# Fewer semaphore updates from TensorE in a two-layer graph network kernel: three a chunk in stage 0 instead of six, one a pair of turns in stage 1

## The chip, the cores and the metric

The kernel runs on one core of a Trainium2 chip. The metric is the time of one execution on the device in microseconds; the kernel before has a median of 1814.22 us in 3 runs. The engines are TensorE (PE, with its weight loads PEld), VectorE (DVE), ScalarE (ACT), GpSimd (POOL) and SyncE (SP, which issues DMAs). Each has an instruction stream of its own, and they keep in step by semaphores: an instruction adds to a semaphore when it is done (`then_inc`), and another engine waits until the semaphore has reached a count (`wait_ge`).

## The reference

Two message-passing layers over 3125 nodes with 64 channels and 100000 edges that are sorted by their destination. Each layer is followed by a sum with its input and a layer norm.

```python
# layer 0
h1, h2, h3, h4 = node_proj(x, W1..W4, b1..b4, node_type)
w5e = einsum('mf,mfh->mh', edge_attr_16, W5[edge_type]) + b5[edge_type]
num = sum(h3[dst] * (h4[src] + w5e), axis=-1)
score = softmax((num / 4)[:, None], axis=-1)[:, 0]   # over an axis of one element
out = h1 + segment_sum(score[:, None] * (h2[src] + w5e), dst)
x = layernorm(x + out)
# layer 1
m = relu(x[src] + edge_attr_32 @ We + be) + 1e-7
ez = exp(m - segment_max(m, dst)[dst])
a = ez / segment_sum(ez, dst)[dst]
x = layernorm(x + ((x + segment_sum(m * a, dst)) @ Wm + bm))
```

## The kernel before

After a setup (node projections, index lists, zeroing of a table in HBM) come two long loops, one for each layer, called stage 0 and stage 1 here. Each goes over 98 chunks. A chunk is 2 x 512 edges: partitions 0 to 63 hold the 64 channels of 512 edges of the first half of the edge list, partitions 64 to 127 those of the second half. Buffers come in pairs; `s = c % 2` picks one and `r = c // 2` counts its uses, so a semaphore `name[s]` reaches `r + 1` when chunk c has signalled.

The order of work on each engine is written out by hand: a `for` over c, and within it a tuple of (work, d), where `d` shifts the chunk that this work is done for. Nothing is reordered by a compiler; an engine whose next instruction waits stands still.

**Stage 0, TensorE** (loop at L934): `pick0` gathers some h rows by one-hot matmuls (L872, three 125x512 bf16 matmuls for each of some 6.9 tiles). `project0` multiplies the edge features by W5 (L881) and adds the gathered h4 rows by transposes into `q_sum` (L854, L859). `turn_inj` transposes the injected h3 rows (L894), `numerator` the products (L909); `difference` adds the other rows to `q_sum` (L854, L859 again), so that this then holds the message part q2; `turn_prob` transposes the widened scores (L918) and `turn_run` the running sums (L927). Each ends with an update: q4_ready, injT, num_ready, q2_ready, probT and runT.

**Stage 0, VectorE** (L1240): `score_parts` of c-1 reduces the turned products (L1184, L1187, L1190); `mask` of c+1 (L1196); `expand` of c is a scan that spreads h3 over the edges (L1205); `products` of c (L1213); `probabilities` of c-1 (L1218 to L1223); `message_sums` of c-2 is a multiplication and a scan (L1229, L1235); `one_hot0` makes about seven one-hot tiles for `pick0` (L1178).

**Stage 0, ScalarE** (L720): `exponents` of c-1, `copy_keep` of c (L690, after the scan of c-2 is done), `widen` of c-1 (L683, what `turn_prob` turns), `copy_q2` of c (L696), at times `copy_picked`, and `store0` of c-2 (L713), which copies the turned running sums out of PSUM and sends them to HBM. GpSimd issues the gathers (`gather0`, L599); eight buffers of a ring are reused once `q2_ready` of the chunk eight back is there.

**Stage 1**: VectorE runs `maxima` (L1328, L1333, L1337), `summands` (L1343), one-hot tiles (L1285) and `sums`, two scans (L1353 and L1358). TensorE picks by one-hot (L970), projects (L949, L952, L958) and then `turn1` turns both running sums: four transposes of the first into the left half of `p_out1`, four of the second into the right half (all L981). ScalarE's `store1` copies the halves out in two instructions (L789), behind `decay` (L776) and ahead of `messages` (L759, L761) of three chunks later.

Of the kernel before, what the change touches and what calls it, by code (L numbers as in the profile page):

```python
# [28 lines left out]
P = 128  # L29
# [50 lines left out]
def gnn_program(nc, t, out):  # L80
# [3 lines left out]
    with ctx:  # L84
# [204 lines left out]
        feat_in, keep_in, inj_in = sems("feat_in"), sems("keep_in"), sems("inj_in")  # L289
        masked, q4_ready, q2_ready, injT = sems("masked"), sems("q4_ready"), sems("q2_ready"), sems("injT")  # L290
        keep_copied, q2_copied, h3_ready, prod_ready = sems("keep_copied"), sems("q2_copied"), sems("h3_ready"), sems("prod_ready")
        num_ready, score_ready, diff_ready = sems("num_ready"), sems("score_ready"), sems("diff_ready")
        exps_ready, prob_ready = sems("exps_ready"), sems("prob_ready")
        softmax_step = sems("softmax_step")
        wide_ready, probT, msg_ready = sems("wide_ready"), sems("probT"), sems("msg_ready")
        run_ready, runT, staged, stored = sems("run_ready"), sems("runT"), sems("staged"), sems("stored")
        s_cut, s_square, s_squared, s_var, s_sqrt, s_x1, s_x1_out = (sem("s_cut"), sem("s_square"), sem("s_squared"),
# [354 lines left out]
        def _(act):  # L652
# [57 lines left out]
            def store0(s, r, c):  # L710
                act.wait_ge(runT[s], r + 1)
                wait(act, stored[s], 16 * r)
                act.activation(stage0[s][:, :, :].rearrange("p j c -> p (j c)"), p_out0[:, :], ACT.Copy).then_inc(staged[s], 1)  # L713
                act.wait_ge(staged[s], r + 1)
                act.dma_start(d_run0[bass.ds(2 * CH * c, 2 * CH), :].rearrange("(p j h) c -> p j (h c)", j=TILES, h=2),
                              stage0[s][:, :, :]).then_inc(stored[s], 16)
# [68 lines left out]
            def store1(s, r, c):  # L785
                act.wait_ge(stored[s], 16 * (EACH + r))
                for q in range(2):
                    act.wait_ge(runT[s], EACH + 2 * r + q + 1)
                    act.activation(stage1[s][:, :, :, q, :], p_out1[:, q * CH:(q + 1) * CH].rearrange("p (j h c) -> p j h c", j=TILES, h=2),  # L789
# [27 lines left out]
        def _(pe):  # L817
# [59 lines left out]
            def project0(s, r, c):  # L877
# [5 lines left out]
                if c in PICKED:  # L883
                    n = PICKED.index(c)
                    pe.wait_ge(own_ready[n // 2 % 2], n // 4 + 1)
                add_rows(s, c, 1).then_inc(q4_ready[s], 1)

# [10 lines left out]
            def difference(s, r, c):  # L898

                pe.wait_ge(prod_ready[s], r + 1)  # L900
                add_rows(s, c, 0).then_inc(q2_ready[s], 1)

            def numerator(s, r, c):
# [4 lines left out]
                for j in range(TILES):  # L908
                    ins = pe.matmul(p_num[:, j * P:(j + 1) * P], prod[s][:, j:CH:TILES], ident[:, :], is_transpose=True,  # L909
                                    start=True, stop=True)  # L910
                ins.then_inc(num_ready[s], 1)

# [9 lines left out]
            def turn_run(s, r, c):  # L922
# [3 lines left out]
                for j in range(TILES):  # L926
                    ins = pe.matmul(p_out0[:, j * P:(j + 1) * P], run[s][:, j:CH:TILES], ident[:, :], is_transpose=True,  # L927
                                    start=True, stop=True)
                ins.then_inc(runT[s], 1)

# [3 lines left out]
            for c in range(-1, CHUNKS - 2):  # L934
                if AHEAD_PIECES + c + 1 < len(PIECES):
                    pick0(AHEAD_PIECES + c + 1)
                for work, d in ((project0, 1), (turn_inj, 1), (numerator, 0), (difference, 0), (turn_prob, -1), (turn_run, -2)):
                    if chunk_of(c + d):
                        work(*chunk_of(c + d))
            for work, back in ((numerator, 2), (difference, 2), (turn_prob, 3), (turn_run, 4), (turn_inj, 1), (project0, 1),  # L940
                               (turn_prob, 2), (numerator, 1), (difference, 1), (turn_run, 3), (turn_run, 2), (turn_prob, 1), (turn_run, 1)):
                work(*chunk_of(CHUNKS - back))
# [32 lines left out]
            def turn1(s, r, c):  # L975
                for q, (src, ready) in enumerate(((run_s[s], s_run[s]), (run_n[s], n_run[s]))):
# [3 lines left out]
                    for j in range(TILES):  # L980
                        ins = pe.matmul(p_out1[:, q * CH + j * P:q * CH + (j + 1) * P], src[:, j:CH:TILES], ident[:, :],  # L981
                                        is_transpose=True, start=True, stop=True)
                    ins.then_inc(runT[s], 1)

# [41 lines left out]
        def _(dve):  # L1026
# [154 lines left out]
            def score_parts(s, r, c):  # L1181

                dve.wait_ge(num_ready[s], r + 1)
                dve.tensor_reduce(score[s][:, :, :, :].rearrange("p j h a -> p (j h a)"), p_num[:, :].rearrange("p (e c) -> p e c", c=C),  # L1184
# [7 lines left out]
            def mask(s, r, c):  # L1192

                dve.wait_ge(feat_in[s], 16 * 4 * (r + 1))
                wait(dve, q4_ready[s], r)
                dve.scalar_tensor_tensor(featm[s][:, :], types[s][:, :], type_of_row[:, :], feat[s][:, :],  # L1196
# [11 lines left out]
            def products(s, r, c):  # L1208

                dve.wait_ge(h3_ready[s], r + 1)  # L1210
                dve.wait_ge(q4_ready[s], r + 1)
                wait(dve, num_ready[s], r)
                dve.scalar_tensor_tensor(prod[s][:, :], h3d[s][:, :], 0.25, q_sum[s], ALU.mult, ALU.mult).then_inc(prod_ready[s], 1)  # L1213
# [11 lines left out]
            def message_sums(s, r, c):  # L1225
# [6 lines left out]
                if c > 0:  # L1232
                    dve.wait_ge(run_ready[1 - s], r + s)
                wait(dve, runT[s], r)
                dve.tensor_tensor_scan(run[s][:, :], keep_late[s][:, :], p_prob[:, :], run[1 - s][:, CH - 1:CH],  # L1235
# [110 lines left out]
            def sums(s, r, c):  # L1346

                first = c == 0
                dve.wait_ge(decay_ready[s], r + 1)
                dve.wait_ge(runT[s], EACH + 2 * r)  # L1350
                if not first:
# [120 lines left out]
```

## Time and profile before

| | us |
|---|---|
| runs, median of 3 (lowest, highest) | 1814.22 (1812.03, 1814.47) |
| profiled execution, span | 2243.3 |
| TensorE matmuls busy | 1756.8 (78%) |
| VectorE busy | 1622.9 (72%) |
| GpSimd busy | 1321.5 (59%) |
| ScalarE busy | 785.0 (35%) |

The profiled execution is one execution under the hardware profiler, and all rows below come from it. It takes 429 us longer than the median of the runs, so a wait seen in it need not be in the runs. Matmuls are pipelined: a busy share of TensorE counts overlapping instructions once, and the end of a matmul is modelled. In a wait, "remote" stands for a releaser that the profile doesn't know, "issue" for a wait in which nothing is shown that the engine waited for.

### The profile page before, as it was taken

Reading aid. Unit: us, or ns where it says so; the run is one execution under the profiler, and the core shown is the slowest. Engines: PE = TensorE matmul, PEld = TensorE weight load, DVE = VectorE, ACT = ScalarE, POOL = GpSimd, SP = SyncE. Lnnn points to the kernel's source line nnn. Section 1 sums busy time; section 2 is a strip of 40 time slices with the busy share of each in tenths; the row PEclk is TensorE's granted clock in tenths of the full one; section 3 lists DMA queues with packets and bytes.
Section 4 is the critical chain, followed back from the end, with each engine's and each line's share of the span. In section 5 each row is a group of like instructions: output and inputs, shape, how many; then the busy total and the mean of one; then the engine's idle time right before and its main releaser. Section 6 shows DMA issues by size and latency. Waiting matters only on the chain.

```text
span 2243.3 us, 28657 instructions
## 1 busy us (share of the span) xinstructions
PE 1756.8 (78%) x8720; PEld 1065.5 (47%) x8720; DVE 1622.9 (72%) x3313; ACT 785.0 (35%) x1508; POOL 1321.5 (59%) x1377
## 2 busy tenths in 40 slices
PE   4447988888788887889875278888888889888864
PEld 4423555555555554555544135444444545445434
DVE  6042777778777777777768558788878878879785
ACT  3110222222222222223222135555545545455551
POOL 5661566666666666666650666666666666666624
PEclk9988998999999999999987579899998999999875
DMA  7951454445454544545443235555545555555441
GB/s 252 342 129 48 124 144 131 146 138 151 135 142 146 141 148 138 148 140 147 139 128 111 53 86 154 149 152 157 157 144 158 161 141 169 150 162 155 142 145 44
DMA packets 216628, 322.18 MB, mean 144 GB/s; under 512 B 62017, under 2 KB 124026, under 8 KB 216347
## 3 DMA queue, kind: packets, MB, share of 16 engines
q1 hardware_dynamic: 128556, 147.55, 22.1%
q0 software_dynamic: 44016, 70.01, 13.6%
q10 hardware_dynamic: 43904, 102.79, 13.0%
q8 instruction: 71, 1.16, 0.2%
q14 instruction: 81, 0.66, 0.1%
HBM read 186.93 MB, written 133.22 MB: 143 GB/s over the span
## 4 chain that ended last, share of the span: by engine, by line
PE 32%; DVE 25%; issue 17%; another core or an unknown queue 15%; ACT 8%; ACTq 1%; POOL 1%; DMA 1%; DVEq 0%; SPq 0%; POOLq 0%
PE wide L970 13%; PE wide L872 5%; DVE h3d L1205 4%; PE wide L981 4%; DVE run L1235 4%; DVE late L1178 4%; DVE edge_lists L1178 3%; DVE score L1184 2%; PE bank L949 2%; DVE prod L1213 2%; ACT block L789 2%; DVE bank L1229 2%; PE bank L958 2%; PE bank L833 1%
## 5 line engine op out<-in xcount | busy, mean ns | idle before, releaser
L609 POOL DMA_INDIRECT rows<-d_x,idx x588 | 558.8, 950 | 323.0 <-issue 154.1
L599 POOL DMA_INDIRECT block<-d_h,idx x496 | 476.4, 960 | 265.0 <-issue 131.4
L970 PE MATMUL wide<-late,ntype_i 125*128 125x512 bf16 x975 | 235.2, 399 | 51.1 <-DVE ntype_i L1318 49.7
L872 PE MATMUL wide<-late,typed 125*128 125x512 bf16 x728 | 234.2, 403 | 39.0 <-issue 19.7
L599 POOL DMA_INDIRECT rows<-d_h,idx x176 | 169.0, 960 | 155.2 <-PE wide L859 51.7
L970 PE MATMUL wide<-edge_lists,ntype_i 125*128 125x512 bf16 x936 | 233.4, 406 | 9.6 <-issue 9.4
L872 PE MATMUL wide<-edge_lists,typed 125*128 125x512 bf16 x672 | 210.8, 395 | 2.8 <-issue 2.7
L981 PE MATMUL wide<-ident,block 128*128 128x128 f32 x784 | 147.3, 317 | 73.1 <-issue 56.5
L789 ACT ACTIVATE block<-wide 128x512 f32<-128x512 f32 x196 | 108.3, 592 | 266.8 <-remote 214.1
L1184 DVE TENSOR_REDUCE score<-bank 128x8 f32<-128x512 f32 x98 | 67.4, 688 | 177.9 <-remote 165.7
L690 ACT ACTIVATE keep_late<-keep 128x512 bf16<-128x512 bf16 x98 | 61.7, 630 | 353.1 <-DVE run L1235 240.8
L970 PEld LDWEIGHTS wide<-late,ntype_i 125*128 125x128 bf16 x975 | 100.1, 103 | 168.6 <-DVE ntype_i L1318 50.1
L696 ACT ACTIVATE q_sb<-wide 128x512 f32<-128x512 f32 x98 | 58.4, 596 | 299.8 <-remote 270.6
L981 PEld LDWEIGHTS wide<-ident,block 128*128 128x128 f32 x784 | 115.9, 210 | 99.6 <-issue 80.4
L970 PEld LDWEIGHTS wide<-edge_lists,ntype_i 125*128 125x128 bf16 x936 | 97.5, 104 | 130.0 <-issue 42.0
L918 PE MATMUL bank<-ident,prob_wide 128*128 128x128 f32 x392 | 67.5, 298 | 113.8 <-issue 84.6
L872 PE MATMUL wide<-late,ntype_i 125*128 125x512 bf16 x364 | 145.4, 400 | 5.4 <-issue 5.2
L872 PEld LDWEIGHTS wide<-late,typed 125*128 125x128 bf16 x728 | 74.4, 103 | 128.4 <-issue 63.0
L872 PE MATMUL wide<-edge_lists,ntype_i 125*128 125x512 bf16 x336 | 132.1, 393 | 2.0 <-issue 2.0
L1205 DVE TENSOR_TENSOR_SCAN h3d<-keep,h3d,bank 128x512 f32<-128x512 bf16 x98 | 124.8, 1274 | 8.7 <-PE bank L894 8.7
L1178 DVE TENSOR_SCALAR late<-msg,pick_of 125x512 bf16<-125x512 f16 x364 | 113.8, 376 | 21.0 <-PE wide L872 10.8
L1333 DVE TENSOR_TENSOR_SCAN h3d<-bank,h3d,keep 128x511 f32<-128x511 f32 x98 | 125.5, 1281 | 3.5
(227 smaller groups left out, 3503.6 us busy)
## 6 DMA issues: line engine op xcount, KB each, us to landing
d_run<-block ACTq DMA_DIRECT2D x98, 512.0 KB
d_inj<-zeros SPq DMA_DIRECT2D x28, 896.0 KB
inj<-d_inj SPq DMA_DIRECT2D x98, 256.0 KB
d_run<-stage ACTq DMA_DIRECT2D x98, 256.0 KB
feat<-in_ea16x3T SPq DMA_DIRECT2D x196, 96.0 KB
types<-d_type SPq DMA_DIRECT2D x196, 64.0 KB
keep<-d_keep SPq DMA_DIRECT2D x196, 64.0 KB
keep<-d_pen SPq DMA_DIRECT2D x196, 64.0 KB
```

What stands on the lines that cost most here:

```text
L599: pool.indirect_dma_start(out=ring[c % RING][:, j, h, :], out_offset=None, in_=d_h24, in_offset=bass.IndirectOffsetOnAxis(ap=idx[:, c, at: ...
L609: pool.indirect_dma_start(out=rows1[c % RING1][:, j, h, :], out_offset=None, in_=d_x1, in_offset=bass.IndirectOffsetOnAxis(ap=idx[:, c, at ...
L789: act.activation(stage1[s][:, :, :, q, :], p_out1[:, q * CH:(q + 1) * CH].rearrange("p (j h c) -> p j h c", j=TILES, h=2), ACT.Copy).then_ ...
L872: ins = pe.matmul(p_pick[s][:, 0:cols], table0[n][:, k, :], hot0[b][:, k - b * KT, 0:cols], start=(k == 0 and n == 0), stop=(k == NT - 1 a ...
L918: ins = pe.matmul(p_prob[:, j:CH:TILES], prob_wide[s][:, j, :, :].rearrange("p h c -> p (h c)"), ident[:, :], is_transpose=True, start=Tru ...
L970: ins = pe.matmul(p_hot[s], table[q][:, SPLIT * k:SPLIT * (k + 1), :].rearrange("p b c -> p (b c)"), hot[s][:, k, :], start=(k == 0 and q ...
L981: ins = pe.matmul(p_out1[:, q * CH + j * P:q * CH + (j + 1) * P], src[:, j:CH:TILES], ident[:, :], is_transpose=True, start=True, stop=True)
L1178: ins = dve.tensor_scalar(hot0[b][:, k - b * KT, 0:cols], pick_slots[u % SLOTS][0:NP, 0:cols], pick_of[:, k:k + 1], None, ALU.is_equal)
L1184: dve.tensor_reduce(score[s][:, :, :, :].rearrange("p j h a -> p (j h a)"), p_num[:, :].rearrange("p (e c) -> p e c", c=C), AX.X, ALU.add) ...
L1205: dve.tensor_tensor_scan(h3d[s][:, :], keep[s][:, :], p_inj[:, :], h3d[1 - s][:, CH - 1:CH], ALU.mult, ALU.add).then_inc(h3_ready[s], 1)
L1235: dve.tensor_tensor_scan(run[s][:, :], keep_late[s][:, :], p_prob[:, :], run[1 - s][:, CH - 1:CH], ALU.mult, ALU.add).then_inc(run_ready[s ...
L1333: dve.tensor_tensor_scan(before[s][:, 1:CH], p_m[c % 3][:, 0:CH - 1], keep[s][:, 1:CH], before[s][:, 0:1], ALU.max, ALU.add).then_inc(befo ...
```

## The change

In stage 0 three kinds of update go from TensorE's stream, or nearly: `num_ready` is dropped, `q4_ready` and `runT` are given for the last chunk alone (as `last_rows` and `last_turned`), so that three a chunk are left (injT, q2_ready, probT). Who waited for one of the dropped waits for a later instruction of the same engine:

- `score_parts` (VectorE) waits for `q2_ready`, so for `difference` as well as `numerator`; `products` waits for `q2_ready` of two chunks back where it waited for `num_ready`, and for `q4_ready` no more (its scan has waited for `injT`, which comes after the rows); `mask` waits for `injT` of two chunks back.
- `message_sums` no longer waits for `runT` of two chunks back.
- `store0` (ScalarE) of a chunk waits for `probT` of the next chunk. For this, TensorE does `turn_run` of c-2 ahead of `turn_prob` of c-1, and in the written-out end of the loop likewise.
- `difference` (TensorE) drops its wait for `prod_ready`, which `numerator` ahead of it has.

In stage 1 `turn1` updates one semaphore after all eight transposes (`turned`) where it updated `runT` after each four; `store1` waits for it once ahead of both copies, and `sums` waits for it. No matmul, copy or DMA is added or removed.

```diff
             def store0(s, r, c):
-                act.wait_ge(runT[s], r + 1)
+                if c == CHUNKS - 1:
+                    act.wait_ge(last_turned, 1)
+                else:
+                    act.wait_ge(probT[1 - s], r + s + 1)
...
             def store1(s, r, c):
                 act.wait_ge(stored[s], 16 * (EACH + r))
+                act.wait_ge(turned[s], r + 1)
                 for q in range(2):
-                    act.wait_ge(runT[s], EACH + 2 * r + q + 1)
...
-                add_rows(s, c, 1).then_inc(q4_ready[s], 1)
+                ins = add_rows(s, c, 1)
+                if c == CHUNKS - 1:
+                    ins.then_inc(last_rows, 1)
...
             def difference(s, r, c):
-                pe.wait_ge(prod_ready[s], r + 1)
                 add_rows(s, c, 0).then_inc(q2_ready[s], 1)
...
             def numerator(s, r, c):
...
-                ins.then_inc(num_ready[s], 1)
...
             def turn_run(s, r, c):
...
-                ins.then_inc(runT[s], 1)
+                if c == CHUNKS - 1:
+                    ins.then_inc(last_turned, 1)
...
-                for work, d in ((project0, 1), (turn_inj, 1), (numerator, 0), (difference, 0), (turn_prob, -1), (turn_run, -2)):
+                for work, d in ((project0, 1), (turn_inj, 1), (numerator, 0), (difference, 0), (turn_run, -2), (turn_prob, -1)):
...
             def turn1(s, r, c):
...
-                    ins.then_inc(runT[s], 1)
+                ins.then_inc(turned[s], 1)
...
             def score_parts(s, r, c):
-                dve.wait_ge(num_ready[s], r + 1)
+                dve.wait_ge(q2_ready[s], r + 1)
...
             def mask(s, r, c):
                 dve.wait_ge(feat_in[s], 16 * 4 * (r + 1))
-                wait(dve, q4_ready[s], r)
+                wait(dve, injT[s], r)
...
             def products(s, r, c):
                 dve.wait_ge(h3_ready[s], r + 1)
-                dve.wait_ge(q4_ready[s], r + 1)
-                wait(dve, num_ready[s], r)
+                if c == CHUNKS - 1:
+                    dve.wait_ge(last_rows, 1)
+                wait(dve, q2_ready[s], r)
...
             def message_sums(s, r, c):
-                wait(dve, runT[s], r)
...
             def sums(s, r, c):
-                dve.wait_ge(runT[s], EACH + 2 * r)
+                wait(dve, turned[s], r)
```

## Rows read from the trace of the kernel before

**Rows 1.** The page: span, and the chain that ended last, by engine.
```profile
span 2243.3 us, 28657 instructions
...
PE 32%; DVE 25%; issue 17%; another core or an unknown queue 15%; ACT 8%; ACTq 1%; POOL 1%; DMA 1%; DVEq 0%; SPq 0%; POOLq 0%
```

**Rows 2.** Windows of the two loops: engines' busy us (instructions), clock, DMA share, GB/s.
```profile
300.00:1100.00 800.00, 688.97 (x3688) 426.11 (x3687) 614.10 (x1384) 221.22 (x471) 506.19 (x527) 0.96 0.49 142
1320.00:2120.00 800.00, 682.01 (x3230) 386.82 (x3228) 647.38 (x1144) 410.18 (x707) 506.26 (x535) 0.91 0.53 153
```

**Rows 3.** The same windows for VectorE's L1184 alone, then for L1353 alone.
```profile
300.00:1100.00 800.00, 53.08 (x77) 0.96 0.49 142
...
1320.00:2120.00 800.00, 111.70 (x88) 0.91 0.53 153
```

**Rows 4.** Waits of stage 0's window: engine, line, releaser, us in total, times, longest.
```profile
ACT q_sb L696 <- remote: 222.3, 68, 6.3
...
DVE score L1184 <- remote: 146.3, 61, 5.4
...
POOL block L599 <- remote: 96.9, 48, 2.6
```

**Rows 5.** Timeline of TensorE's matmuls: start us, us, engine, line, count, idle before.
```profile
611.53 1.02 PE L881 MATMUL wide<-featm,w 128*128 128x512 f32 x2
...
612.97 0.60 PE L894 MATMUL bank<-ident,inj 128*128 128x128 f32 x4
613.40 0.64 PE L909 MATMUL bank<-ident,prod 128*128 128x128 f32 x4
613.88 0.52 PE L854 MATMUL wide<-ident,block 128*128 128x128 f32 x3
614.24 0.39 PE L859 MATMUL wide<-typed,ident 128*128 128x128 f32 x2
616.87 0.66 PE L918 MATMUL bank<-ident,prob_wide 128*128 128x128 f32 x4 [2.24 <-issue]
617.36 0.65 PE L927 MATMUL bank<-ident,run 128*128 128x128 f32 x4
617.85 0.38 PE L872 MATMUL wide<-edge_lists,typed 125*128 125x512 bf16 x1
```

**Rows 6.** Timeline of VectorE, the chunk that follows.
```profile
618.57 0.69 DVE L1184 TENSOR_REDUCE score<-bank 128x8 f32<-128x512 f32 x1 [0.89 <-remote]
619.29 0.16 DVE L1187 TENSOR_REDUCE top<-score 128x8 f32<-128x8 f32 x1
...
621.55 0.69 DVE L1213 SCALAR_TENSOR_TENSOR prod<-h3d,wide 128x512 f32<-128x512 f32 x1
622.15 0.15 DVE L1218 TENSOR_REDUCE total<-expo 128x8 f32<-128x8 f32 x1
...
623.39 1.28 DVE L1235 TENSOR_TENSOR_SCAN run<-keep_late,run,bank 128x512 f32<-128x512 bf16 x1
624.59 2.17 DVE L1178 TENSOR_SCALAR late<-msg,pick_of 125x512 bf16<-125x512 f16 x7
```

**Rows 7.** Timeline of ScalarE and GpSimd at the same place.
```profile
615.67 0.63 ACT L690 ACTIVATE keep_late<-keep 128x512 bf16<-128x512 bf16 x1 [4.43 <-DVE run L1235]
...
618.64 0.60 ACT L696 ACTIVATE q_sb<-wide 128x512 f32<-128x512 f32 x1 [1.82 <-remote]
...
618.87 0.94 POOL L599 DMA_INDIRECT block<-d_h,idx  x1 [1.83 <-remote]
```

**Rows 8.** Timeline of TensorE in stage 1: the turns of a chunk, then the picks.
```profile
1703.61 1.13 PE L981 MATMUL wide<-ident,block 128*128 128x128 f32 x8
...
1704.58 4.70 PE L970 MATMUL wide<-late,ntype_i 125*128 125x512 bf16 x21
```

**Rows 9.** Waits of stage 1's window.
```profile
ACT block L789 <- remote: 207.4, 53, 8.1
...
DVE h3d L1328 <- ACT bank L761: 96.3, 17, 9.3
```

More of the change, by code:

```diff
@@ L289, in gnn_program @@
         feat_in, keep_in, inj_in = sems("feat_in"), sems("keep_in"), sems("inj_in")
-        masked, q4_ready, q2_ready, injT = sems("masked"), sems("q4_ready"), sems("q2_ready"), sems("injT")
+        masked, q2_ready, injT, last_rows = sems("masked"), sems("q2_ready"), sems("injT"), sem("last_rows")
         keep_copied, q2_copied, h3_ready, prod_ready = sems("keep_copied"), sems("q2_copied"), sems("h3_ready"), sems("prod_ready")
-        num_ready, score_ready, diff_ready = sems("num_ready"), sems("score_ready"), sems("diff_ready")
+        score_ready, diff_ready = sems("score_ready"), sems("diff_ready")
         exps_ready, prob_ready = sems("exps_ready"), sems("prob_ready")
@@ L295, in gnn_program @@
         wide_ready, probT, msg_ready = sems("wide_ready"), sems("probT"), sems("msg_ready")
-        run_ready, runT, staged, stored = sems("run_ready"), sems("runT"), sems("staged"), sems("stored")
+        run_ready, staged, stored = sems("run_ready"), sems("staged"), sems("stored")
+        last_turned, turned = sem("last_turned"), sems("turned")
         s_cut, s_square, s_squared, s_var, s_sqrt, s_x1, s_x1_out = (sem("s_cut"), sem("s_square"), sem("s_squared"),
@@ L908, in numerator @@
                 for j in range(TILES):
-                    ins = pe.matmul(p_num[:, j * P:(j + 1) * P], prod[s][:, j:CH:TILES], ident[:, :], is_transpose=True,
-                                    start=True, stop=True)
-                ins.then_inc(num_ready[s], 1)
+                    pe.matmul(p_num[:, j * P:(j + 1) * P], prod[s][:, j:CH:TILES], ident[:, :], is_transpose=True,
+                              start=True, stop=True)
             def turn_prob(s, r, c):
@@ L936, in _ @@
                     pick0(AHEAD_PIECES + c + 1)
-                for work, d in ((project0, 1), (turn_inj, 1), (numerator, 0), (difference, 0), (turn_prob, -1), (turn_run, -2)):
+                for work, d in ((project0, 1), (turn_inj, 1), (numerator, 0), (difference, 0), (turn_run, -2), (turn_prob, -1)):
                     if chunk_of(c + d):
                         work(*chunk_of(c + d))
-            for work, back in ((numerator, 2), (difference, 2), (turn_prob, 3), (turn_run, 4), (turn_inj, 1), (project0, 1),
-                               (turn_prob, 2), (numerator, 1), (difference, 1), (turn_run, 3), (turn_run, 2), (turn_prob, 1), (turn_run, 1)):
+            for work, back in ((numerator, 2), (difference, 2), (turn_run, 4), (turn_prob, 3), (turn_inj, 1), (project0, 1),
+                               (turn_run, 3), (turn_prob, 2), (numerator, 1), (difference, 1), (turn_run, 2), (turn_prob, 1), (turn_run, 1)):
                 work(*chunk_of(CHUNKS - back))
```

## The prediction

> **What bounds the kernel now.** I read the page first, then the two chunk loops by windows, then their waits, then one chunk of each in the timeline. The page [rows 1] has a span of 2243.3 us for the profiled execution, while the runs have a median of 1814.22: the profiled execution is 429 us, or 24%, longer. Its chain of waits gives "another core or an unknown queue" 15% (336 us) and "issue" 17% (381 us). So the first question is which of the waits seen there are in the runs at all. The windows [rows 2] show the two loops: TensorE is busy 86% of stage 0 and VectorE 77%; in stage 1 they are 85% and 81%. The counts in [rows 3] give the chunk time: 800/77 = 10.4 us in stage 0 (one L1184 a chunk) and 800/88 = 9.1 us in stage 1 (one L1353 a chunk).
>
> The waits of stage 0 [rows 4] say where the rest of a chunk goes. VectorE stands 146.3 us before the score reduction L1184, ScalarE 222.3 us before its copy L696, and the queue of gathers 96.9 us, all released by "remote". The timeline shows one such case. The numerator's transposes L909 start at 613.40 and last 0.64, so they end at 614.04; the difference block ends at 614.24 + 0.39 = 614.63 [rows 5]. VectorE waits for the first block's signal, ScalarE and GpSimd for the second's, and they go on at 618.57, 618.64 and 618.87 [rows 6, 7]: 4.5 us after the first block and about 4 us after the second, within 0.3 us of each other, though TensorE itself had stood idle for 2.24 us in between. TensorE's signals thus come late and in bunches in the profiled execution. This is what the change aims at.
>
> Are they late in the runs too? An estimate: stage 0 has 98 chunks of 10.4 us, and one chunk of VectorE's own work is 8.2 us, from 618.57 to 624.59 + 2.17 = 626.76 [rows 6]. TensorE's own work is 4.47 for the picks (20.7 matmuls at 0.216, which is (4.70 - 0.38)/20 of the 21 in [rows 8]), 1.87 from L881 to L909 (611.53 to 613.40), 1.06 for numerator and difference, 0.98 for the two turns (616.87 to 617.85) [rows 5], in all 8.4 us. Going from 10.4 to 8.4 us in stage 0 saves 98 x 2.0 = 196 us. Stage 1 at VectorE's 647.38/88 = 7.4 us of busy time instead of 9.1 [rows 2, 3] saves 98 x 1.7 = 167. Together 2243 - 363 = 1880 us, still 66 us over the median, and whatever a run has around its span only widens that. So the runs have no room for late signals of this size: without tracing, both loops go at the pace of the engines' own work, TensorE and VectorE within 0.2 us of each other in stage 0, VectorE in stage 1.
>
> **The change part by part.** *Fewer signals.* Three of six updates a chunk go in stage 0 (294, less two that stay for the last chunk) and one of two in stage 1 (98). Does an update hold up TensorE? L909's four transposes with one update take 613.88 - 613.40 = 0.48, or 0.12 each; L854's three without any take 614.24 - 613.88 = 0.36, also 0.12 each; L894's four with one take 0.43 [rows 5]. An update costs TensorE's stream under 0.01 us: 392 x 0.01 = at most 4 us, and I take 0, since TensorE's stream is what the rows time. The Trainium skill says otherwise of completions: "TensorE: Matmul & The Clock Gate", section "The cost: per-tile semaphore tail", has increments serialize at 26.3 ns each. By it the 392 removed would be worth up to 10 us, were each the last thing waited for. The rows show no such cost in issue; what they show of arrival is priced as a rival.
>
> *Fewer waits.* VectorE loses two waits a chunk (L1211, L1234) and TensorE one (L900). VectorE's idle time in the chunk of the timeline is the 0.89 us before L1184; none is printed at L1213 or L1235, before which the removed waits stand [rows 6]. These waits are taken while the operation before them runs, so I take 0. The cover is that operation; without it a wait could cost VectorE the 0.03 us that lie between L1184's end (619.26) and L1187's start, which waits for it [rows 6]: 98 x 2 x 0.03 = 6 us. Bounds 0 and 6 us of gain.
>
> *The score waits for the second block.* L1184 now waits for the difference too, which ends 614.63 - 614.04 = 0.59 us after the numerator [rows 5]. If VectorE were already standing there each time, that is 98 x 0.59 = 58 us. Is it? From the end of a message scan L1235 (R), VectorE has its one-hot tiles until R + 2.09 (624.67 to 626.76) [rows 6]. TensorE, counted from the scan before, does: keep copy and widening 1.30 (from ScalarE's start at 615.67 to TensorE's at 616.87 is 1.20 [rows 7, 5]; I allow 0.10 from the scan's end), two turns 0.98, picks 4.47, project and inj 1.87, numerator 0.64: 9.26 us. With a chunk of 8.2 to 8.4 us that is R + 0.9 to R + 1.1, so the score has 1.0 to 1.2 us to spare. With the difference it has 0.4 to 0.6, and the next part gives back most of what is lost.
>
> *turn_run ahead of turn_prob.* Both need the scan of chunk c-2, but turn_prob also needs ScalarE's widening, 1.2 us later. In the case in the rows TensorE stood 2.24 us before L918 and then did L927's 0.49 us behind it [rows 5]. With the order swapped these 0.49 us fall into the wait. The whole round that goes through both engines and covers two chunks is: 1.30 + 0.98 + 4.47 + 1.87 + 0.64 on the way to the score, and 6.10 on VectorE from 618.57 to the scan's end at 624.67 [rows 6], 15.36 us. After the change it is 15.36 - 0.49 + 0.59 = 15.46, or 7.7 us a chunk in both. It is below 8.2 and 8.4, so it doesn't bind, and the two edits are worth 0.05 us a chunk against each other even where it does (5 us of loss). With signals late by some 2.7 us twice a round it comes to 20.8, or 10.4 us a chunk: that is how the profiled execution gets its pace.
>
> *store0 waits for probT of the next chunk.* turn_prob of c-1 now directly follows turn_run of c-2, and the pair ends when it did. Nothing is added: ScalarE is busy 221/77 = 2.9 us of a chunk [rows 2, 3], and what is queued behind store0 is the exponents, which VectorE wants 3.6 us after the score begins (622.15) [rows 6]. The mask's wait for injT instead of q4 is for two chunks back: 0.
>
> *Stage 1.* store1's first copy now waits for all eight turns L981, not for four; they take 1.13 us, so it starts up to 0.5 us later [rows 8]. Behind it on ScalarE stand the second copy, the store's DMA and messages of c+2; VectorE waits for those only two chunks later. ScalarE is busy 410.18/88 = 4.7 us of a chunk that has at least 7.4, so 0.5 fits into 2.7 of slack: 0. Without that cover it is 98 x 0.5 = 49 us. [rows 9] show that this cover can fail when signals are late: 207.4 us of "remote" before L789 sit beside 96.3 us in which VectorE waits for ScalarE's L761.
>
> Sum for the runs: 0 to -4 for the updates, 0 to -6 for the waits, and +5 to -5 for the swap with the later score; stage 1 0. I take -1 us: 1813. For the profiled execution the sum is made against its own 2243 us: it is bound by late signals, so fewer of them may shorten the bunches, and I expect 2180 to 2250.
>
> **The rivals.** *Signals are late in the runs as well, only less (faster).* In the bunch of the rows VectorE goes on at 618.57 and ScalarE at 618.64, for two successive signals: 0.07 us between them [rows 6, 7]. Three fewer in stage 0 are 0.2 us a chunk, 20 us if all are in front of the one waited for, 10 if half are: 1804. For it: the bunches are there in every part of the trace. Against it: the 1880 us above.
>
> *Updates serialize as such (faster).* If every removed update would have ended a wait about 0.03 us later, the gap between dependent operations in [rows 6], 392 x 0.03 = 12 us: 1802. It is the mechanism of the serializing rule of the Trainium skill named above. Against it: the same 0.12 us a transpose with and without an update.
>
> *The score's later release becomes the bound (slower).* Place: VectorE before L1184. It decides from the point at which the difference ends after R + 2.09, that is if TensorE runs more than 0.4 us later against VectorE than counted, as when it never waits at turn_prob and the swap gives nothing back. Then a chunk loses up to 0.59 us. Where TensorE itself is the bound its pace is unchanged, so it is only chunks in which VectorE is, say a fifth: 20 x 0.59 = 12 us, 1826; all would be 1872. For it: TensorE's 8.4 and VectorE's 8.2 are so near that small differences decide. Against it: the round of 15.46.
>
> *ScalarE's late start in stage 1 reaches VectorE (slower).* A third of 49 us: 1830. Against it: 2.7 us of slack.
>
> *The change is no saving at all*, since what releases the signals isn't their number: then the forecast's own time.
>
> **How the numbers follow.** Forecast 1813, own range 1808 to 1817: 0.53. Late signals 1804: 0.20. Serializing 1802: 0.05. Later score 1826: 0.17. Stage 1, 1830: 0.05. A measurement of this kernel can tell 0.2%, 3.6 us, from no change. Faster by more: 0.25 and a little of the forecast's own range, 0.27. Slower: 0.22. Same: 0.51. The range from 1799 to 1826 takes in the first rivals and the nearer half of the slower ones.
>
> **What would show it.** Right: in the changed trace L909, L854 and L859 keep 0.12 us a transpose; "remote" stays the releaser before L1184 and L696; L927 comes before L918 and lies within TensorE's wait; VectorE's busy time a chunk is unchanged; the runs stay within 4 us. Wrong: if the runs drop by over 10 us together with the profiled span, signals were late in the runs too; if idle before L1184 grows and its releaser is the difference block L859, the later score decides; if the wait before L1328 for L761 grows, it was stage 1.

## The result, and the profile after

The changed kernel takes 1817.2 us (median of 15 runs, 1814.72 to 1820.94) beside 1813.82 us before (15 runs, 1812.03 to 1816.28): a ratio of 1.0019, with a 95% interval of 1.0012 to 1.0025. It is slower by 3.4 us: a small change, under the 3.6 us that were called the limit of what can be told from no change, but its interval doesn't reach 1. Forecast was 1813, 1 us the other way, with 1808 to 1817 as the forecast's own range.

The page of the changed kernel: span, busy us of each engine, and the chain that ended last by engine.

```profile
span 1813.8 us, 28558 instructions
PE 1631.2 (90%) x8720; PEld 1028.8 (57%) x8720; DVE 1627.4 (90%) x3313; ACT 791.9 (44%) x1508; POOL 1318.4 (73%) x1377
...
PE 40%; POOL 37%; issue 13%; DMA 4%; DVE 3%; SPq 3%; ACT 1%; ACTq 0%; DVEq 0%; POOLq 0%
```

The span is 430 us below that of [rows 1], though the runs differ by 3 us, and no releaser of another core or an unknown queue is left. That isn't the change's doing. The kernel before, run and profiled once more (a0_same below), gave this page:

```profile
span 1808.8 us, 28657 instructions
PE 1624.9 (90%) x8720; PEld 1025.1 (57%) x8720; DVE 1629.2 (90%) x3313; ACT 784.3 (43%) x1508; POOL 1318.1 (73%) x1377
...
POOL 42%; PE 38%; issue 14%; DMA 2%; DVE 2%; ACT 1%; SPq 0%; ACTq 0%; POOLq 0%; DVEq 0%
```

This kernel runs at one of two speeds. The experiments below were five jobs, each on a chip of its own. In three of them the kernel before takes about 1814 us; in the two others it has medians of 2244.08 and 2272.5 us, its single runs lie between 2239 and 2280, and the profiles taken there show TensorE's signals late as in [rows 4 to 7]. The profile that the prediction read looks like those, the times beside it like the others. "On time" and "late" name the two from here on. Each chip had only one job, so whether the speed belongs to the chip or to something else in the job isn't shown. A ratio always compares runs on one chip; profiles are compared within one kind.

With signals on time, windows of stage 0 in the changed kernel and in the kernel before (a0_same) answer [rows 2]: length; busy us (instructions) of PE, PEld, DVE, ACT and POOL; clock, DMA share, GB/s.

```profile
300.00:800.00 500.00, 500.00 (x2908) 327.25 (x2907) 481.51 (x1088) 177.30 (x368) 379.74 (x395) 1.00 0.62 177
```

```profile
300.00:800.00 500.00, 500.00 (x2911) 327.81 (x2910) 482.93 (x1091) 177.42 (x369) 379.39 (x396) 1.00 0.62 177
```

TensorE is busy for all of 500 us in both, at a granted clock of 1.00 (2.4 GHz). It is the bound of the steady part of stage 0, and it has no wait there into which anything could be moved.

Where did 3.4 us go? The starts of the score reduction of the 3rd, the 80th and the last of the 98 chunks, kernel before (a0_same) and then changed kernel:

```profile
174.18 0.68 DVE L1184 TENSOR_REDUCE score<-bank 128x8 f32<-128x512 f32 x1
...
807.30 0.69 DVE L1184 TENSOR_REDUCE score<-bank 128x8 f32<-128x512 f32 x1
...
948.09 0.66 DVE L1184 TENSOR_REDUCE score<-bank 128x8 f32<-128x512 f32 x1
```

```profile
174.36 0.68 DVE L1189 TENSOR_REDUCE score<-bank 128x8 f32<-128x512 f32 x1
...
808.34 0.69 DVE L1189 TENSOR_REDUCE score<-bank 128x8 f32<-128x512 f32 x1
...
952.00 0.67 DVE L1189 TENSOR_REDUCE score<-bank 128x8 f32<-128x512 f32 x1
```

The 77 steady chunks take 633.12 us before and 633.98 after, 8.22 and 8.23 each; the last 18 take 140.79 and 143.66. Between these two profiles 0.9 us is spread over the steady chunks and 2.9 us lies at the end of stage 0. The first number holds up in all ten profiles of on-time kernels (below), the second doesn't. This profile of a0_same was its fastest run (1810.61 us, with a median of 1813.32), and the other profiles in which the score waits for the numerator, fewer_gathers apart, have 141.0 to 144.0 us for the last 18 chunks. What VectorE waited for in those last chunks (engine, line, releaser, us in total, times, longest), before and after:

```profile
DVE score L1184 <- PE bank L909: 6.8, 5, 5.1
```

```profile
DVE score L1189 <- PE wide L863: 8.5, 3, 6.5
...
DVE score L1189 <- PE wide L858: 0.8, 2, 0.6
```

The releaser before was the numerator (L909); after, it is the difference block (L858, L863 in the changed file), as it must be. The waits are 9.3 us and not 6.8, but swap_only_3 below, which keeps the old wait, has 8.8: the sum at the end doesn't separate the kernels. Over the whole of stage 0 it does: VectorE is idle before the score for 14.3 us in a0_same and for 21.7 in the changed kernel.

### The profile page after: what moved, and what is told of

It reads as the page before. It is cut to its first block, busy times and chain, and to the rows that moved or that the text cites. A ratio compares the mean times of both kernels' runs of the same rounds, so it can differ in the third digit from the quotient of the medians.

```text
span 1813.8 us, 28558 instructions
## 1 busy us (share of the span) xinstructions
PE 1631.2 (90%) x8720; PEld 1028.8 (57%) x8720; DVE 1627.4 (90%) x3313; ACT 791.9 (44%) x1508; POOL 1318.4 (73%) x1377
## 4 chain that ended last, share of the span: by engine, by line
PE 40%; POOL 37%; issue 13%; DMA 4%; DVE 3%; SPq 3%; ACT 1%; ACTq 0%; DVEq 0%; POOLq 0%
POOL rows L610 31%; PE wide L876 20%; PE wide L885 4%; PE wide L858 4%; POOL block L600 3%; PE bank L931 2%; PE bank L914 2%; PE bank L922 2%; PE bank L900 2%; DMA d_inj<-zeros 1%; SPq L451 1%; POOL d_inj L620 1%; POOL typed L630 1%; PE bank L830 1%; PE wide L863 1%
## 5 line engine op out<-in xcount | busy, mean ns | idle before, releaser
L600 POOL DMA_INDIRECT block<-d_h,idx x496 | 482.6, 973 | 151.2 <-issue 150.3
L975 PE MATMUL wide<-late,ntype_i 125*128 125x512 bf16 x975 | 221.0, 382 | 49.7 <-DVE ntype_i L1323 49.7
L876 PE MATMUL wide<-late,typed 125*128 125x512 bf16 x728 | 220.4, 385 | 18.9 <-DVE late L1183 18.8
L975 PE MATMUL wide<-edge_lists,ntype_i 125*128 125x512 bf16 x936 | 209.9, 379 | 0.0
L876 PE MATMUL wide<-edge_lists,typed 125*128 125x512 bf16 x672 | 200.0, 379 | 0.1
L986 PE MATMUL wide<-ident,block 128*128 128x128 f32 x784 | 142.4, 306 | 37.6 <-DVE block L1363 29.5
L986 PEld LDWEIGHTS wide<-ident,block 128*128 128x128 f32 x784 | 110.2, 209 | 61.9 <-DVE block L1363 47.7
L876 PE MATMUL wide<-late,ntype_i 125*128 125x512 bf16 x364 | 139.8, 384 | 0.0
L780 ACT ACTIVATE bank<-prob_wide 128x512 f32<-128x512 f32 x98 | 59.0, 602 | 179.2 <-DVE block L1363 176.5
L1338 DVE TENSOR_TENSOR_SCAN h3d<-bank,h3d,keep 128x511 f32<-128x511 f32 x98 | 125.5, 1281 | 3.5
L1240 DVE TENSOR_TENSOR_SCAN run<-keep_late,run,bank 128x512 f32<-128x512 bf16 x98 | 125.5, 1280 | 3.5
L876 PE MATMUL wide<-edge_lists,ntype_i 125*128 125x512 bf16 x336 | 127.3, 379 | 0.0
L1358 DVE TENSOR_TENSOR_SCAN block<-bank,block 128x512 f32<-128x512 f32 x98 | 124.3, 1268 | 0.8 <-ACT bank L780 0.8
L1363 DVE TENSOR_TENSOR_SCAN block<-bank,block,run 128x512 f32<-128x512 f32 x98 | 122.7, 1252 | 0.0
```

Of the source, the lines that this page charges most:

```text
L600: pool.indirect_dma_start(out=ring[c % RING][:, j, h, :], out_offset=None, in_=d_h24, in_offset=bass.IndirectOffsetOnAxis(ap=idx[:, c, at: ...
L876: ins = pe.matmul(p_pick[s][:, 0:cols], table0[n][:, k, :], hot0[b][:, k - b * KT, 0:cols], start=(k == 0 and n == 0), stop=(k == NT - 1 a ...
L975: ins = pe.matmul(p_hot[s], table[q][:, SPLIT * k:SPLIT * (k + 1), :].rearrange("p b c -> p (b c)"), hot[s][:, k, :], start=(k == 0 and q ...
L1338: dve.tensor_tensor_scan(before[s][:, 1:CH], p_m[c % 3][:, 0:CH - 1], keep[s][:, 1:CH], before[s][:, 0:1], ALU.max, ALU.add).then_inc(befo ...
L1358: dve.tensor_tensor_scan(run_s[s][:, :], p_decay[:, :], expm[s][:, :], run_s[1 - s][:, CH - 1:CH], ALU.mult, ALU.add).then_inc(s_run[s], 1)
L1363: dve.tensor_tensor_scan(run_n[s][:, :], p_decay[:, :], mexp[s][:, :], run_n[1 - s][:, CH - 1:CH], ALU.mult, ALU.add).then_inc(n_run[s], 1)
```

## The experiments

**The kernel before, again, and the two halves.** a0_same is the kernel before. s0_only has stage 0's part alone, s1_only stage 1's:

```diff
@@ s1_only, against before: store1, turn1, sums
+                act.wait_ge(runT[s], EACH + r + 1)
                 for q in range(2):
-                    act.wait_ge(runT[s], EACH + 2 * r + q + 1)
...
-                    ins.then_inc(runT[s], 1)
+                ins.then_inc(runT[s], 1)
...
-                dve.wait_ge(runT[s], EACH + 2 * r)
+                dve.wait_ge(runT[s], EACH + r)
```

> The kernel before, unchanged: what two equal kernels differ by, and a second profile of it. Theory A (the late signals of the profiled execution are an accident of that one execution, or of tracing, and not of the number of updates): ratio 1.000, and a profiled span near the runs' 1812 us, with stage 0 at about 8.2 us a chunk. Theory B (six updates a chunk are more than tracing can follow, three are not): ratio 1.000, but the profiled span again far above the runs, about 2240 us, with VectorE and ScalarE released by remote.

Measured: 1813.32 us, ratio 0.9999 (0.9990 to 1.0008), and a span of 1808.8 us. Theory B is gone: six updates a chunk don't by themselves make signals late.

> Only stage 0's part of the change; stage 1 again has two updates a chunk and a wait before each of the two copies. Theory 'later score or stage 0' (the 3.4 us are lost in stage 0, where VectorE's score now also waits for the difference block): ratio 1.0019, 1817 us. Theory 'stage 1' (ScalarE's copies start up to 0.5 us later): ratio 1.000, 1814 us.

Measured: 1816.71 us, 1.0020 (1.0011 to 1.0029). Stage 0's part alone can make the whole difference; its interval also allows half of it.

> Only stage 1's part. Theory 'stage 0': 1.000, 1814 us, stage 1 at the same 7.39 us a chunk as in the changed kernel. Theory 'stage 1': 1.0019, 1817 us.

Measured: 1816.06 us, 1.0012 (1.0003 to 1.0021), neither the one nor the other. It was repeated on another chip.

> Only stage 1's part again; it had 1.0012 (1.0003 to 1.0021) while the profiles show 724 to 726 us for stage 1 with it and without it. Theory 'stage 1 costs nothing': 1.000, within 0.1%. Theory 'stage 1 costs 2 us': 1.001.

Measured: 1815.61 us, 1.0008 (0.9999 to 1.0017), beside the theories' 1.000 and 1.001. In stage 1's window from 1040 to 1690 us the trace shows ScalarE's new wait, before (a0_same) and in s1_only_2:

```profile
ACT bank L776 <- DVE block L1358: 199.3, 87, 2.9
...
ACT block L789 <- PE wide L981: 1.7, 2, 1.3
```

```profile
ACT bank L776 <- DVE block L1358: 168.1, 87, 2.5
...
ACT block L789 <- PE wide L981: 18.8, 63, 1.6
```

ScalarE stands before store1's copy in 63 chunks, 0.3 us each, 17 us more than before, and its wait for the scan is 31 us shorter: the 0.5 us of later start fit into its slack, as costed. VectorE has no listed wait in this window with either kernel. From the first scan of stage 1 to the end of its last, the four on-time profiles with one signal take 724.0 to 726.5 us and the seven with two 723.6 to 726.4. So no place in the trace shows a cost, but the ratios do lean to one: 1.0012, whose interval leaves out 1.000, and 1.0008, whose interval just takes it in; together about 1.001, or 2 us. Whether stage 1's part costs that where signals are on time stays open.

**The score's own wait back.** num_back is the changed kernel with `num_ready` restored for the score alone:

```diff
+                ins.then_inc(num_ready[s], 1)
...
-                dve.wait_ge(q2_ready[s], r + 1)
+                dve.wait_ge(num_ready[s], r + 1)
```

> The changed kernel, but the numerator updates its own semaphore again and the score waits for that one: four updates a chunk in stage 0. Theory 'later score': the idle time of VectorE before the score, 21.7 us in stage 0 of the changed kernel, falls by some 8 us or more and the time goes back to 1814 us, ratio 1.000. Theory 'order or store0' (turn_run ahead of turn_prob, store0 behind probT): stays at 1.0019, 1817 us, with the idle time before the score as it was.

Measured: 1815.24 us, 1.0008 (0.9999 to 1.0017), between the two theories, and 633.07 us for the 77 steady chunks, as before the change. VectorE's idle time before the score falls from 21.7 to 12.7 us, the 8 us or more that were expected. By the medians about half of the loss comes back; what is left is within the error.

**One part alone each.** swap_only is the kernel before with turn_run ahead of turn_prob in the loop and in its end. score_later is the kernel before with one wait changed, and old_end the changed kernel with the old order in the last chunks:

```diff
@@ swap_only, against before
-... (difference, 0), (turn_prob, -1), (turn_run, -2)):
+... (difference, 0), (turn_run, -2), (turn_prob, -1)):
@@ score_later, against before
-                dve.wait_ge(num_ready[s], r + 1)
+                dve.wait_ge(q2_ready[s], r + 1)
@@ old_end, against the changed kernel: the written-out end as before; store0
@@ waits for last_turned in the last four chunks; and
-                if c == CHUNKS - 1:
+                if c >= CHUNKS - 4:
                     ins.then_inc(last_turned, 1)
```

Their first job got a chip where signals are late (before: 2272.5 us), so did the second (another chip, 2244.08 us), and the third, without old_end, got one where they are on time (1814.15 us).

> The kernel before with turn_run ahead of turn_prob alone, in the loop and in the written-out end; all six updates stay. The clean profiles put stage 0's steady chunks at 8.22 us in both kernels and the loss into what follows the last gather: 15.6 and 17.2 us from the last gather's end to the last message scan with the old order, 19.0 and 18.9 with the new. Theory 'end': this run is slower by 1 to 3 us, ratio 1.001 to 1.002, and has 18 to 19 us there. Theory 'score' (the score's wait for the difference does it): ratio 1.000 and 15 to 17 us.

Measured, late: 0.9978 (0.9966 to 0.9990).

> As put on record for the first run of this kernel, which got a chip with late signals. Where signals are on time, theory 'end': 1.001 to 1.002, with 18 to 19 us from the last gather's end to the last message scan; theory 'score': 1.000 and 15 to 17 us.

Measured, late again: 1.0002 (0.9986 to 1.0018). The same edit on the first late chip had 0.9978, with an interval that doesn't meet 1: late ratios of one edit differ between jobs by more than a single interval tells, so one late ratio by itself carries little.

> Where signals are on time (the kernel before near 1814 us): theory 'end', that the new order of turn_run and turn_prob costs the 3 us behind the last gather: 1.001 to 1.002, 18 to 19 us from the last gather's end to the last message scan. Theory 'score', that the score's wait for the difference costs them: 1.000 and 15 to 17 us. Where signals are late (near 2250 us): as measured twice, 0.998 to 1.000.

Measured, on time: 1814.34 us, 1.0001 (0.9992 to 1.0010). Theory "end" falls: the new order costs nothing that can be told. The second sign was the time from the last gather's end to the end of the last message scan: 17.15 us here, above the 15 to 17 us of theory "score" and below the 18 to 19 of theory "end".

> The kernel before with one wait changed: the score waits for the difference block and not for the numerator; six updates, old order. Theory 'score': 1.001 to 1.002. Theory 'end': 1.000. Steady chunks stay at 8.2 us in both, since TensorE has no idle time there, and VectorE's idle time before the score rises from 14.3 us.

Measured, late: 1.0006 (0.9993 to 1.0020).

> Where signals are on time, theory 'score': 1.001 to 1.002. Theory 'end': 1.000, 15 to 17 us behind the last gather, and 8.2 us a steady chunk.

Measured, late again: 1.0028 (1.0014 to 1.0041).

> Where signals are on time: theory 'score' 1.001 to 1.002, theory 'end' 1.000 with 15 to 17 us behind the last gather. Where they are late: 1.0006 and 1.0028 were measured, so 1.002.

Measured, on time: 1816.71 us, 1.0010 (1.0001 to 1.0019). The steady 77 chunks take 633.90 us, against 633.12 in a0_same and 632.98 in swap_only_3. The three profiles in which the score waits for the difference (after, s0_only, score_later_3) have 633.8 to 634.0, the seven that keep the old wait 633.0 to 633.5. From the last gather's end to the last scan the three have 18.9 to 19.2 us, though score_later_3 has the old order, and the old wait 15.6 to 18.6 (fewer_gathers left out). Again without fewer_gathers, the means are 633.14 us for the steady chunks and 142.4 for the last 18 with the old wait, and 633.89 and 143.4 with the new one: 0.75 and 1.05 us more, 1.8 in all, of which only the first part is clear of the spread.

> The changed kernel with the old order in the written-out end of stage 0 (the last four chunks' turn_run signal store0 directly, so that this is allowed). Theory 'end': 1.000 to 1.0005, 15 to 17 us behind the last gather. Theory 'score': as the changed kernel, 1.0015 to 1.002 and 19 us.

Measured, late: 1.0016 (1.0000 to 1.0031).

> Where signals are on time, theory 'end': 1.000 to 1.0005, 15 to 17 us behind the last gather. Theory 'score': 1.0015 to 1.002, 19 us.

Measured, late: 2257.47 us, 1.0057 (1.0034 to 1.0081). The old end doesn't help there; it was not run where signals are on time, which is where its expectation was stated.

> The changed kernel again, on whatever chip this job gets. There are two kinds so far: one where the kernel before takes 1814 us and signals are on time, one where it takes 2272 us and TensorE's signals come late. On the first kind all theories give 1.0019 again. On the second: theory 'fewer signals help late signals' gives 0.99 or less (2250 us or less); theory 'the release and not the count sets the time' gives 1.000 within 0.2%.

Measured, late: 2256.05 us, 1.0043 (1.0024 to 1.0061). Neither theory (0.99 or less; 1.000 within 0.2%) had this: where fewer signals should have helped, the change costs 10 to 12 us. The score's later wait alone has 6 us of them on this chip (score_later_2, 1.0028). The wait it was meant to shorten is still there, in the window 300 to 1100 us:

```profile
DVE score L1189 <- remote: 156.5, 70, 4.4
```

against 146.3 us in [rows 4], and VectorE gets 1369 instructions into that window, not more than the 1384 of [rows 2]. Stage 1, from its first scan (L1338; L1333 before) to the end of its last (L1363; L1358), in after_2 and in swap_only_2, which has stage 1 as before:

```profile
1317.78 1.28 DVE L1338 TENSOR_TENSOR_SCAN h3d<-bank,h3d,keep 128x511 f32<-128x511 f32 x1
...
2195.57 1.26 DVE L1363 TENSOR_TENSOR_SCAN block<-bank,block,run 128x512 f32<-128x512 f32 x1
```

```profile
1306.42 1.28 DVE L1333 TENSOR_TENSOR_SCAN h3d<-bank,h3d,keep 128x511 f32<-128x511 f32 x1
...
2177.66 1.26 DVE L1358 TENSOR_TENSOR_SCAN block<-bank,block,run 128x512 f32<-128x512 f32 x1
```

That is 879.0 us with one signal for both turns and 872.5 with two; on this chip the two other kernels have 877.8 (old_end_2, one signal) and 873.5 (score_later_2, two). The 4 to 7 us would fit store1 waiting for the later of two late signals, which isn't shown: these are four single profiles on one chip, and on the first chip with late signals old_end had 891.3 and the three with two signals 885.8 to 892.7.

**The suspected wait made longer.** score_latest lets the score also wait for the turn_prob block behind the difference:

```diff
-                dve.wait_ge(num_ready[s], r + 1)
+                dve.wait_ge(q2_ready[s], r + 1)
+                if c > 0:
+                    dve.wait_ge(probT[1 - s], r + s)
```

> The kernel before, but the score of a chunk waits for the difference block and, behind it, for the turn_prob block of the chunk before: the suspected wait taken further by 0.5 us or more. Theory 'score': each place where VectorE stands before the score costs more again, and in steady chunks the spare time ahead of the score runs out: slower than score_later, 1.003 or more where signals are on time, 1.005 or more where they are late. Theory 'the 0.1% of score_later is noise': 1.000 to 1.001.

Measured, on time (before: 1813.98 us): 1826.33 us, 1.0075 (1.0062 to 1.0089). The wait in its last chunks, from the window 865 to 965 us:

```profile
DVE score L1186 <- PE bank L918: 18.7, 9, 2.5
```

The steady chunks now take 638.8 us for 77, 5.7 more than in a0_same, and the last 18 take 149.5, 8.7 more (7.1 more than the old wait's mean). The step from the numerator to the difference costs 1.8 us (0.0010 x 1814), the step from there to turn_prob 11.8 (0.0065 x 1814). It has only 5 runs, but they lie within 3 us of each other, over 9 us above the highest of 26 before. So the score's wait does move the time, in the steady chunks as well as at the end.

**What an update costs.** more_signals is the kernel before with updates on twelve more transposes a chunk, to a semaphore that nobody reads:

```diff
+                    if j < TILES - 1:
+                        ins.then_inc(extra, 1)
```

> The kernel before with 12 more updates a chunk in stage 0 (the first three of each four transposes in the inj, numerator, turn_prob and turn_run blocks add to a semaphore that nobody waits for), 1176 in all; it prices one update. Theory 'an update is free in TensorE's stream': ratio 1.000, at most 1.001. Theory 'updates serialize': at the 0.03 us put on record, 1176 x 0.03 = 35 us, ratio 1.019. And theory B, that many updates disturb the profiled execution: a span of 2100 us or more beside runs at 1814.

Measured, late: 2280.14 us, 1.0040 (1.0026 to 1.0054): 9 us over 1176 updates, or 0.008 us each if the updates are what costs it; this is one late ratio and was not repeated. As the kernel before has the same late signals on that chip, this says nothing for theory B.

> 12 more updates a chunk, 1176 in all. It was 1.0040 on a chip with late signals (9 us, 0.008 us an update). Where signals are on time: 1.000 if an update is free, 1.019 if each costs 0.03 us.

Measured, on time: 1813.60 us, 0.9998 (0.9989 to 1.0007), with 633.12 us for the steady chunks. By the upper end of the interval an added update costs less than 0.0011 us (0.0007 x 1814 / 1176). Where signals are on time the change had nothing to save by dropping 390 of them.

**The gather queue.** In fewer_gathers 38 chunks miss one gather each, so part of the rows is stale:

```diff
+        def left_out(c):
+            return int(c >= RING and c not in PICKED)
...
-                    for j in range(tiles_of(c)):
+                    for j in range(tiles_of(c) - (h * left_out(c))):
```

> The kernel before with one gather left out (its rows stay those of an earlier chunk) in each of the 38 chunks from the eighth on that pick no tile by one-hot: 38 x 1.25 us less on GpSimd's queue, so that part of the gathered rows is not read anew. The queue has no pause in stage 0 where signals are on time, and VectorE stands 5.1 us before a score near the end. Theory 'the gathers set the end of stage 0': that wait and the shorter ones go, 4 to 10 us, ratio 0.995 to 0.998. Theory 'TensorE sets all of it': 1.000.

Measured, on time: 1809.24 us, 0.9975 (0.9965 to 0.9984), as theory "the gathers set the end" had it. The releaser of GpSimd's idle time between 145 and 935 us in a0_same:

```profile
POOL block L599 <- issue: 141.4, 464, 0.3
POOL rows L599 <- issue: 48.8, 160, 0.3
```

That is 0.3 us after each gather, and besides only two waits of 0.3 us for TensorE: 0.97 (the mean of L599) + 0.3 = 1.27 us a gather without a pause, 6.9 a chunk, so 8.7 us a chunk beside TensorE's 8.2. The chunks that were gathered ahead cover the difference until the loop's end. There TensorE has no more picks to do, a chunk could take 6 us (926.08 to 932.13 below), and the rows aren't there yet. TensorE, which adds them by L854, and then VectorE's scores in a0_same:

```profile
923.21 1.13 PE L854 MATMUL wide<-ident,block 128*128 128x128 f32 x4 [5.39 <-DMA block<-d_h,idx]
924.13 1.06 PE L894 MATMUL bank<-ident,inj 128*128 128x128 f32 x4
924.98 1.06 PE L909 MATMUL bank<-ident,prod 128*128 128x128 f32 x4
```

```profile
914.69 0.69 DVE L1184 TENSOR_REDUCE score<-bank 128x8 f32<-128x512 f32 x1 [0.55 <-PE bank L909]
926.08 0.69 DVE L1184 TENSOR_REDUCE score<-bank 128x8 f32<-128x512 f32 x1 [5.09 <-PE bank L909]
932.13 0.67 DVE L1184 TENSOR_REDUCE score<-bank 128x8 f32<-128x512 f32 x1
```

The wait of 5.39 us for the rows becomes the 5.09 us before the score. After it four transposes take 1.06 us, at a granted clock of 0.50 (1.2 GHz) from 923 to 926 us, where they take 0.64 at 1.00 in the steady chunks. Over 880 to 965 us the clock is 0.84 in a0_same and 0.81 in the changed kernel; what that adds to the end wasn't separated.

With 38 gathers fewer the last one starts at 900.28 and not at 937.47 us, none of the last eight scores waits, and the last 18 chunks take 137.1 us.

## Why the prediction was wrong

*The runs have no late signals.* Right for the chips of the times: a clean profile's chunk is 8.2 us in stage 0 against the 8.2 to 8.4 that were worked out from the engines' own work. What wasn't thought of is that untraced runs can be late too: in two of five jobs they were.

*An update costs TensorE under 0.01 us; taken as 0.* Right: 0.9998 with 1176 more, which stand just ahead of the updates that are waited for, so under 0.0011 us each on time. The serializing rival (1802) falls with it. The Trainium skill's rule ("TensorE: Matmul & The Clock Gate", section "The cost: per-tile semaphore tail", 26.3 ns an increment) is stated there for a group of small tiles that run side by side. No run here has such tiles; for the whole-array transposes of this kernel it doesn't show as time (0.9998). The rival of signals a little late in the runs (1804) falls as well: the on-time profiles list no "remote" wait before the score, and the change made nothing faster.

*TensorE stands before turn_prob L918 until the widening is there.* This is the step that failed. Two terms of the sum rest on it: the 0.49 us that turn_run ahead of turn_prob was to give back, and the 1.0 to 1.2 us that the score was to have to spare. The wait of 2.24 us was a row from a late profile. On time the same place looks like this, TensorE and then VectorE in a0_same:

```profile
312.70 0.64 PE L909 MATMUL bank<-ident,prod 128*128 128x128 f32 x4
313.18 0.64 PE L854 MATMUL wide<-ident,block 128*128 128x128 f32 x4
313.66 0.60 PE L918 MATMUL bank<-ident,prob_wide 128*128 128x128 f32 x4
314.10 0.64 PE L927 MATMUL bank<-ident,run 128*128 128x128 f32 x4
```

```profile
310.26 1.28 DVE L1235 TENSOR_TENSOR_SCAN run<-keep_late,run,bank 128x512 f32<-128x512 bf16 x1
...
312.94 0.82 DVE L1178 TENSOR_SCALAR late<-msg,pick_of 125x512 bf16<-125x512 f16 x2
313.68 0.67 DVE L1184 TENSOR_REDUCE score<-bank 128x8 f32<-128x512 f32 x1
```

No idle time stands before L918, so the order of L918 and L927 is worth nothing (swap_only_3, 1.0001). This term alone would only have moved the forecast to about no change.

*The score has 1.0 to 1.2 us to spare, 0.4 to 0.6 with the difference.* Wrong by 0.7 to 0.9 us here, and this is the term that makes the change a loss. In the rows above the numerator ends at 312.70 + 0.64 = 313.34 and the score starts at 313.68: 0.34 us. The difference ends at 313.82, 0.14 us after that start. Over the 3rd to the 80th chunk of a0_same the median between the numerator's end and the score's start is 0.23 us, and in 61 of the 78 the difference ends only after that start (median of all 78: 0.35 us after it). The count took TensorE as leaving the widening as soon as it was there, but in the steady chunks TensorE, the bound, doesn't wait there and comes later: its numerator ends at R + 1.80 in these rows and not at R + 0.9 to 1.1. So the point that the slower rival named (difference later than R + 2.09) is passed: R is 310.26 + 1.28 = 311.54, and 313.82 is R + 2.28. The rival was right in mechanism and too large in number. It priced 20 chunks at 0.59 us. In steady chunks TensorE is the bound, and VectorE's later start is absorbed but for 0.01 us each, 0.8 to 0.9 us in all. At stage 0's end, where TensorE is out of picks and waits for rows, more is paid: 1.05 us by the means of the profiles, 2.9 between the two shown first, but kernels with the old wait spread over 140.8 to 144.0 us there, so that part isn't sized. In the runs the score's wait alone measures 1.8 us (1.0010, 1.0001 to 1.0019). The sign that the prediction had named for this rival appeared: idle time before the score grew, released by the difference block.

*Stage 1 costs nothing.* Open: 1.0012 and 1.0008 for that part alone, no place in the trace. Where signals are late it may cost some 6 us on one chip; on the other it doesn't show.

*The fewer waits on VectorE are free, store0 costs nothing.* Nothing in the traces speaks against it; they weren't tried alone. They are the one other place for the loss that num_back left standing.

*The profiled execution takes 2180 to 2250 us.* Wrong for a late one: after_2 has a span of 2261.7, on a chip where the kernel before has a median of 2244.08.

Of the 3.4 us, 1.8 are the score's wait by the direct test and 2.0 by taking it back (1.0019 less 1.0008). The other 1.5 are not placed: stage 1's part (about 2 us by its two ratios) would make them up, and so would store0's later wait, but s0_only, with 1.0020, leaves nothing for stage 1; each of these ratios has an error of 1.6 us. What was left out altogether is the gather queue. The prediction took the gathers for a consumer that waits (96.9 us in [rows 4]), and costed the loop by TensorE and VectorE alone; so it had no term for the last chunks, where the rows run out. That the queue costs time there is shown (fewer_gathers, 4.5 us); how much of this change's loss lies there isn't.

## What to carry to other kernels

Price a later release by the slack that the bound engine's real position leaves, read from a profile whose span agrees with the runs; if the two disagree by 24%, get another profile before using any of its waits. Hanging a consumer on a later signal of the same producer saved an update that cost under 0.0011 us here, and gave up slack that was only about a quarter of a microsecond. And look at the end of each loop by itself: a queue that runs without a pause, here the gathers, can set it even when another engine sets the steady pace.

## What the runs showed of the hardware

The same kernel takes 1814 us on three chips and 2244 and 2273 us on two others, one job on each. In the late profiles, instructions of VectorE, ScalarE and GpSimd that wait for TensorE go on several us after the block they wait for, three engines within 0.3 us of each other (4.5 to 4 us in [rows 5 to 7]), and all the "remote" waits of [rows 4] stand before instructions that wait for TensorE. Halving TensorE's signals in stage 0 doesn't cure it (1.0043). What releases the waiting engines there was not found.

On time, 1176 more updates on TensorE's transposes gave a ratio of 0.9998 (0.9989 to 1.0007), under 0.0011 us each. GpSimd's gathers follow each other with 0.3 us between them for 624 gathers, with only two other waits between them, 1.27 us from one to the next in the mean. After TensorE had waited 5.39 us for rows, its granted clock was 0.50 from 923 to 926 us, and four 128x128 transposes took 1.06 us where they took 0.64 at a clock of 1.00.
